# A fused attention and feed-forward kernel: a sixth split value tile, one side task in an earlier slot, and transposes moved from TensorE to DMA

## What is computed

```python
x = x + tanh(g_xattn) * attention(layernorm(x), ctx)
x = x + tanh(g_ffn) * ffn(layernorm(x))

# attention: 16 heads, everything through low-rank latents
q_big  = einsum(hidden_q @ Wq.T, w_kc_q)            # per head 384
q_r    = q_big @ W_qr;  k_r = rope(kv_c) @ W_kr     # per head 64
attn   = softmax(q_r @ k_r.T)                       # 512 x 1024 per head and batch
ctx_c  = attn @ rope(kv_c)                          # values are the 128-wide latents
out    = (ctx_c @ w_kc_kv) @ Wo.T

# ffn: three quantized products of 512 x 2048
xq = round(rmsnorm(x) * scale)     # int8 range, a scale per row
wq = round(tanh(w / mean|w|))      # -1, 0, 1
h  = silu(xq1 @ wq1.T) * (xq2 @ wq2.T)
y  = quant(rmsnorm(h)) @ wq3.T
```

## Time and profile before

| | |
|---|---|
| median of three runs | 655.0 us |
| the profiled execution, its own time | 656.19 us |
| its span, first to last instruction | 654.4 us |
| PE busy | 635.1 us, 97% |
| DVE busy | 536.5 us, 82% |
| ACT busy | 422.2 us, 65% |
| POOL busy | 360.2 us, 55% |
| granted TensorE clock | 1.000 throughout (the upper level, 2.4 GHz) |
| DMA: share of 16 engines in attention, in the feed-forward part | 0.77 to 0.83, 0.03 to 0.08 |

### The profile page before, as it was taken

One profiled execution on the slowest core, in us unless ns is written; L12 is line 12 of the kernel. 1 busy time (PEld: TensorE's weight loads), 2 busy tenths in 40 slices (PEclk: granted clock), 3 DMA queues, 4 the chain that ended last, 5 costly groups with the idle time before them and its releaser, 6 DMA issues.

```text
span 654.4 us, 9986 instructions
## 1 busy us (share of the span) xinstructions
PE 635.1 (97%) x2968; PEld 394.0 (60%) x2968; DVE 536.5 (82%) x870; ACT 422.2 (65%) x693; POOL 360.2 (55%) x304
## 2 busy tenths in 40 slices
PE   8789999999999999999999999999999998999997
PEld 7555466766766676666666666566656554545553
DVE  4778787788878877887789978997899987998863
ACT  2564686477737764776567766776666633598875
POOL 4722376655545554565367854664457144686651
PEclk9999999999999999999999999999999999999999
DMA  8207976788589858984988798878689872000001
GB/s 283 87 6 188 274 196 164 206 223 240 151 227 241 219 131 239 251 224 106 251 222 221 201 242 224 222 195 231 169 221 251 198 177 81 1 1 33 17 35 48
DMA packets 45208, 112.79 MB, mean 172 GB/s; under 512 B 11888, under 2 KB 15088, under 8 KB 45040
## 3 DMA queue, kind: packets, MB, share of 16 engines
q1 hardware_dynamic: 42128, 104.24, 60.1%
q10 hardware_dynamic: 2976, 8.06, 4.0%
q0 software_dynamic: 64, 0.00, 0.0%
HBM read 45.16 MB, written 2.10 MB: 72 GB/s over the span
## 4 chain that ended last, share of the span: by engine, by line
PE 68%; DVE 10%; SPq 8%; ACT 4%; issue 4%; DMA 3%; POOL 1%; PEld 1%; POOLq 0%; ACTq 0%; DVEq 0%; PEldq 0%
PE ps_s L1443 11%; SPq L1132 8%; PE ps_b L1476 6%; PE ps_s L623 5%; PE ps_ctx L1476 5%; PE ps_b L1339 4%; PE ps_b L1394 4%; DMA G<-E 3%; PE ps_b L1341 3%; PE ps_b L1413 3%; PE ps_b L1340 3%; ACT E L1675 2%; PE ps_b L674 2%; DVE small L1858 2%; PE ps_ctx L1472 2%
## 5 line engine op out<-in xcount | busy, mean ns | idle before, releaser
L1675 ACT ACTIVATE E<-ps_s,small 128x1024 f32<-128x1024 f32 x128 | 142.5, 1116 | 143.4 <-DVE small L1858 110.5
L1241 POOL TENSOR_TENSOR G_lo<-G,g_hi 128x512 fp32r<-128x512 f32 x130 | 168.0, 1306 | 117.7 <-ACT g_hi L1619 117.7
L1858 DVE TENSOR_REDUCE small<-ps_s 128x1 f32<-128x1024 f32 x128 | 149.8, 1211 | 34.5 <-PE ps_s L1443 34.3
L1872 DVE STREAM_TRANSPOSE E<-E 128x1024 f32<-128x1024 f32 x124 | 152.0, 1230 | 0.1
L1199 POOL TENSOR_SCALAR E<-E,small 128x1024 f32<-128x1024 f32 x64 | 78.9, 1233 | 109.6 <-DVE small L1864 98.0
L1619 ACT ACTIVATE g_hi<-G 128x512 fp32r<-128x512 f32 x130 | 76.9, 631 | 3.5 <-DVE wq L1888 3.5
L1339 PE MATMUL ps_b<-b_hi,ctx_hi 128*128 128x512 f32 x128 | 66.8, 522 | 0.3 <-DVE ctx_lo L1818 0.3
L1476 PE MATMUL ps_b<-G,kv 128*128 128x512 f32 x126 | 63.7, 600 | 1.7 <-DMA G<-E 1.7
L1476 PE MATMUL ps_ctx<-G,kv 128*128 128x512 f32 x126 | 64.6, 607 | 0.1
L1443 PE MATMUL ps_s<-k_hi,q_hi 64*128 64x512 f32 x256 | 57.3, 444 | 3.8 <-ACT E L1675 2.6
L623 PE MATMUL ps_s<-wq,q12T 128*128 128x512 fp8e4 x256 | 59.8, 379 | 0.1
(11 more groups left out here) (203 smaller groups left out, 1211.7 us busy)
## 6 DMA issues: line engine op xcount, KB each, us to landing
G<-E SPq DMA_DIRECT2D x496, 128.0 KB, 2.6
w_stage<-in_wffn SPq DMA_DIRECT2D x37, 512.0 KB, 4.8
w_stage<-in_wffn ACTq DMA_DIRECT2D x11, 512.0 KB, 4.4
wo_s<-in_woT SPq DMA_DIRECT2D x8, 512.0 KB, 5.4
wq_s<-in_wq SPq DMA_DIRECT2D x7, 512.0 KB, 5.5
wkcq_s<-in_wkcqT SPq DMA_DIRECT2D x7, 384.0 KB, 3.4
out<-x_sb SPq DMA_DIRECT2D x8, 256.0 KB, 2.0
x_sb<-in_x SPq DMA_DIRECT2D x3, 512.0 KB, 6.3
```

The costliest lines, as they stand in the source:

```text
L1241: nc.gpsimd.tensor_tensor(g_tile(w % 2, i, G_lo), tile, high_part(i).bitcast(F32).rearrange("p (t i q) -> p t i q", t=ST, i=4), ALU.subtra ...
L1675: nc.scalar.activation(out, scores, ACT.Exp, bias=negmax[:, k:k + 1], accum_out=rowsum[:, k:k + 1]).then_inc(exp_done, 1)
L1858: nc.vector.tensor_reduce(negmax[:, k:k + 1], ps_s[:, t % 2, :], AX_X, ALU.max, negate=True).then_inc(max_done, 1)
L1872: nc.vector.transpose(e_tile(w % 2, t), e_tile(w % 2, t)).then_inc(blocks_turned, 1)
```

## The change

- `SPLIT` is 6: tile 5 is split too, so that 26 more plain products become split ones. Tiles 6 and 7 are taken first. The fourth high part (index 3) is made at step 2 and no longer at step 3, that is between the exponentials of steps 2 and 3; GpSimd makes its low part before the second scaling. With six parts in three places, the wait for the unit before moves to part 2.
- The side task `("m",)` of pairs 1 to 6 moves to unit 2, step 2 of the pair before, as `("m", 1)`. `("a",)` moves from step 2 to step 0 of unit 0 and `("k", 1, 1)` from step 2 to step 0 of unit 2. Pair 0 does both `("m",)` and `("m", 1)`, pair 6 (`"late"`) and pair 7 none. VectorE takes the low part of a task of step 0 behind its two maxima for `("a",)` and `("k", 1, 1)` too, as it did for `q` (`behind`).
- SyncE no longer waits for `("m",)` at a pair's start (it finished a unit earlier), and waits after the exchange of unit 1 until it has landed (`landed`), before it issues the weight loads behind it. The weight sums of unit 1 stand at steps 3 and 4, not 1 and 4.
- In the feed-forward part the rows of tiles 2 to 7 and the hidden tiles 0 to 5 are transposed by DMA. ScalarE first converts int16 to bf16 in place (`widen_rows`, 128 x 1024; `widen_hidden`, 128 x 2048), then SyncE issues one transposing DMA. `down(t - 3)` follows chunk 1 of step `t`, in place of `down(t - 2)` at the end; the read of it stands ahead of the fourth product. The last two hidden tiles are still turned by TensorE.
- Small tiles are packed closer to make room, and the bf16 identity is made at the start.

```diff
-SPLIT, PLACES = 5, 3
-STEP_TILE = (5, 6, 0, 1, 7, 2, 3, 4)
-HIGH_STEPS = (0, 0, 0, 3, 4)
+SPLIT, PLACES = 6, 3
+STEP_TILE = (6, 7, 0, 1, 2, 3, 4, 5)
+HIGH_STEPS = (0, 0, 0, 2, 3, 4)
...
 SIDE = [
-    {0: ("m",), 2: ("a",), 3: ("k", 0, 0), 4: ("out", 3, 0), 5: ("out", 3, 1), 6: ("b", 0), 7: ("b", 1)},
+    {0: ("a",), 3: ("k", 0, 0), 4: ("out", 3, 0), 5: ("out", 3, 1), 6: ("b", 0), 7: ("b", 1)},
     {0: ("q", 0), 1: ("k", 0, 1), 4: ("out", 0, 0), 5: ("out", 0, 1), 7: ("k", 1, 0)},
-    {2: ("k", 1, 1), 4: ("out", 1, 0), 5: ("out", 1, 1)},
+    {0: ("k", 1, 1), 2: ("m", 1), 4: ("out", 1, 0), 5: ("out", 1, 1)},
     {0: ("q", 1), 4: ("out", 2, 0), 5: ("out", 2, 1)},
 ]
...
+        def landed(sp, p, w):
+
+            sp.wait_ge(exchanged[w % 2], 2 * EXCHANGE * p + EXCHANGE * (w // 2 + 1))
+            sp.sem_inc(sp_passed, 1)
...
                 if not (variant == "last" and w == 3):
                     exchange(sp, *unit_ahead(p, w, 1))
+                    if w == 0 and variant != "last":
+                        landed(sp, *unit_ahead(p, w, 1))
...
                 if splits(p, w):
                     split_low(pool, p, w, 2)
+                    split_low(pool, p, w, 3)
...
                 if splits(p, w):
-                    split_low(pool, p, w, 3)
                     split_low(pool, p, w, 4)
+                    split_low(pool, p, w, 5)
...
+            def turn_rows(t):
+                sp.wait_ge(q12_wide, t - FIRST_MOVED + 1)
+                sp.wait_ge(up_done, HC * (t - 1))
+                sp.dma_start_transpose(q12T[:, t % 2, :, :, :].rearrange("p i c s -> p (i c) s"),
+                                       qn12[:, t % 2, :, :].rearrange("p i d -> p (i d)").bitcast(BF16)).then_inc(q12_moved[t % 2], 16)
+
+            def turn_hidden(t):
+                sp.wait_ge(q3_wide, t + 1)
+                if t >= 2:
+                    sp.wait_ge(mm3_done, t - 1)
+                sp.dma_start_transpose(q3T[:, t % 2, :, :], qn3[:, t % 2, :].bitcast(BF16)).then_inc(q3_moved[t % 2], 16)
+
+            for t in range(1, TT):
+                if t + 1 < TT:
+                    turn_rows(t + 1)
+                if t >= 2:
+                    turn_hidden(t - 2)
+                if t >= 4:
+                    store(t - 4)
...
+        def widen_hidden(act, t):
+
+            act.wait_ge(q3_ready, t + 1)
+            rows = qn3[:, t % 2, :]
+            copy_act(rows.bitcast(BF16), rows).then_inc(q3_wide, 1)
...
                 if t == 1:
                     silu(act, 2, 0, 0)
+                    widen_hidden(act, 0)
                     norm_act(act, 2, 0)
-                elif mm:
+                else:
+                    widen_hidden(act, t - 1)
                     hidden_square(act, t, k)
...
                 if mm and t > 2:
                     product(dve, t, k, 2)
                     chunk_max(dve, t, k, 1)
+                    down_read(t - 3)
                     product(dve, t, k, 3)
```

More of the change, by code:

```diff
@@ L134 @@
 XN_JOIN_SLOTS = ((4, 1), (4, 2), (4, 3), (5, 0))
-def side_tasks(w, first, last):
-    def wanted(task):
-        before = task[:2] == ("out", 3)
-        behind = task[0] in ("m", "a", "k", "q")
-        return not (first and before or last and behind)
-    return {c: task for c, task in (LAST_SIDE_TASKS if last else SIDE)[w].items() if wanted(task)}
 PROLOGUE_TASKS = [("m",), ("a",), ("k", 0, 0), ("k", 0, 1), ("q", 0, 0), ("q", 0, 1), ("k", 1, 0), ("k", 1, 1), ("q", 1)]
@@ L1918, in dve_pair @@
                     ctx_low(dve, *((p, w - 1) if w else (p - 1, 3)))
-                if not queries:
+                if not behind:
                     low(1)
```

234 lines of the change are left out of this document (118 added, 116 removed).

## The result

| | before | the change |
|---|---|---|
| median | 655.1 us (four runs, 654.8 to 655.5) | 661.9 us (four runs, 658.2 to 665.0) |
| ratio | | 1.0109, 95% interval 1.0078 to 1.0139 |
| profiled execution, its span | 656.19, 654.4 us | 661.89, 660.1 us |
| granted TensorE clock of the four runs | 1.000 (profiled) | 0.992, 0.990, 0.997, 0.992 (at 661.9, 665.0, 658.2 and 662.0 us) |

What follows compares the result with a forecast made beforehand. TensorE was taken to bound, with VectorE close behind at `q` in attention and a four-engine loop nearly as long in feed-forward. Attention -5.2 and feed-forward +4.1 gave -1.1 on 656.2, 654.0 us on the median; range 650.3 to 664.

Steps and rivals of the forecast that it cites:

- Rival C: Feed-forward loop does not lengthen (term +1.5, not +4) or attention gives -7 to -9: 650 to 652.7 us; chance 0.27.
- TensorE idle 1 to 2 us a step: Expected sign in feed-forward tiles 3 to 5: TensorE waits this long, released by VectorE's products and not by a DMA.
- The copy between two exponentials makes the second of them some 0.5 us later: Attention, sixth split tile: ScalarE's extra copy delays an exponential; the 26 splits were to save TensorE 4.2 us.
- Rival B: Attention gives less: late low parts make 26 units wait 0.1 to 0.2 us each, attention -1, 656.5 to 659; chance 0.23.
- the join before pair 7: Join of six value tiles before attention's last pair: up to 0.9 us later, under VectorE's 2 us of work, costed at nothing.
- -3.0 for pair 2: Attention, pair 2 start to `q`: -1.6 as in other pairs, plus 1.4 us lost to the exchange of unit 1.
- `q` 17.5 us after the start: Attention, unit 1: TensorE's product `q` comes 17.5 us after the pair's start in place of 19.1, set by VectorE.
- +0.95 in unit 2: Attention, pairs 1 to 5: moved `m` adds 1.43 us on TensorE's path, the splits of three other units take 0.48.
- the lower bound of -9: Attention's best case if no wait is left at `q`: -5.2 less 4 x 0.4 and 2 x 1.1 us.
- the turns cost nothing: Feed-forward transposing DMAs: 4 to 5 us a row turn, 5 to 6 a hidden turn; up to 6 us a row turn is free.
- rival A: Slow row turns in SyncE's queue make `gate_up` wait for `q12T` from 6 us a turn on: 661 to 668 us; chance 0.20.
- The upper bound of attention: Attention's worst case: VectorE gains nothing in unit 0, `q` stays, unit 2 costs its 0.95 five times: about +4 us.

Runs made afterwards that it cites:

- c_ends: The change with plain instead of transposing transfers, down product behind the fourth chunk and its read at step end (not tile 7), widening ahead of the squares: 1.0099 of before.
- c_gaps: The change with plain transfers, down product and read at step ends, widening of hidden tiles 1 to 4 in halves behind second and third silu: 656.3 us, 1.0027 of before.
- c_widen_late: The change with plain transfers and the hidden widening moved behind the squares; the read stays ahead of the fourth product: 1.0113 of the kernel before.
- c_ends_wide: The change with plain transfers, the hidden widening behind the squares, and down product and read at the ends of their steps: 1.0176 of the kernel before.
- att_only: The kernel before with the changed attention and packed tiles, feed-forward part as before: 654.6 us, 0.9999 of the kernel before.
- att_again: The kernel before with the changed attention, feed-forward part as before, run once more on another chip: 654.6 us, 1.0000 of the kernel before.

## Why the prediction was wrong

The terms as forecast, and as the profile of the change has them against the one they were made on:

| term | forecast | measured |
|---|---|---|
| pairs 1 to 6, start to `q` | -10.6 | -9.1 |
| `q` to the next start, pairs 0 to 5 | +5.9 | +5.6 |
| behind the `q` of pair 6 | -0.5 | +1.5 |
| **attention** | **-5.2** | **-1.9** |
| first widening, tile 2 | +1.3, +1.4 | +1.4, +1.5 |
| tiles 3 to 5 | +2.0 | +3.5, of it 1.45 the clock |
| tile 6 | +1.1 | +3.05, of it 1.5 the clock |
| tile 7 | -1.7 | -1.8 |
| **feed-forward** | **+4.1** | **+7.7** |
| **sum on the profiled execution** | **-1.1** | **+5.7** (with 0.1 in what is left) |

- **Right: the mechanism of the feed-forward part.** Taking 8.1 us from TensorE gained nothing, because a loop over four engines was within 0.1 us of it; the change lengthened that loop to 12.2 us a tile, by the widening and by the early read. `c_ends` shows that the widening alone is enough (12.1), `c_gaps` that with both out the loop is back at 11.56. The early read alone comes to 12.2 by the 0.66 us between `c_widen_late` and `c_ends_wide`; no run has it by itself. Rival C, that it would not lengthen, fell.
- **Wrong: "TensorE idle 1 to 2 us a step" was costed at nothing.** The forecast saw the waits and asked only what they delay. The waits were 2.1 to 2.4 us, in one piece, at the first chunk of a tile. Behind three of them the clock fell, and behind two of these the step grew, by 1.45 and 1.51 us in the profiled execution. This is the larger part of what the feed-forward sum lacked (2.96 of 3.6 us).
- **Wrong: 'The copy between two exponentials makes the second of them some 0.5 us later', with GpSimd's extra subtraction costed at nothing because it waits for 45% of the time.** That is a share of the whole span. At four places the low part is the last thing that TensorE waits for, 0.4 to 1.1 us each. Rival B named this, with 0.1 to 0.2 us in each of 26 units and attention at -1; attention came to -1.9 by the trace, and to no gain in the time of `att_only` and `att_again`. It came as few waits in few units: 0.5 us in pair 1, 0.4 in pair 5, 1.6 in pair 6. Behind the `q` of pair 6 the forecast had -0.5, and it was +1.5.
- **Wrong: the join before pair 7, "up to 0.9 us later, under VectorE's 2 us of work".** TensorE waits 0.75 us for it. The forecast had it covered by VectorE's work, but the one who waits is TensorE.
- **Wrong: -3.0 for pair 2, carried over to the median.** Against the profiled execution it measured -2.9. But 1.4 of it was a wait for an exchange that the second trace of the same kernel does not have, so that it is no gain on the median. A transfer's delay in one pair out of three equal ones should have been read as that execution's.
- **Right by luck: `q` 17.5 us after the start** (17.6 in pairs 2 to 4, 18.4 in 5 and 6, and 18.4 in pair 1, which has 0.51 of waiting in it), +0.95 in unit 2 (0.8 to 1.1). But the forecast got it by following VectorE, put TensorE at `q` after 17.1, and kept a wait there. None is recorded but 0.07 to 0.08 us in pairs 5 and 6. The earlier trace rows have no wait in pair 1 either, so that TensorE's own 19.1 less 1.43 and 0.16 gives the same 17.5: the number was TensorE's, not VectorE's, and the lower bound of -9, made of waits to be removed, had nothing under it.
- **Right: the turns cost nothing.** 3.2 and 4.4 us, below the 4 to 5 and 5 to 6 taken, and both under their cover; rival A did not occur. The Trainium skill ("VectorE: DVE Perf Modes", The three transpose paths) gives 1309 ns a block; the trace has 8 blocks in 3.2 us and 16 in 4.4, so the blocks do not go one after another at that price. The Trainium skill's rule that a transposing DMA is as fast as a plain one ("Advanced Engine Details and Errata", X-Bar Transpose) is nearer, but not met here: 1.4 times as long.
- **Two slips of reckoning.** The upper bound of attention, "about +4", is 5 x 0.95 + 1.1 - 0.5 = +5.4 by its own terms. Rival A speaks of 18 separate block transposes a step; a step has 8 + 16 = 24 blocks, and 18 is the number of groups of eight in the whole part. Neither moved the sum.

So the sum missed by 6.8 us: 3.3 in attention, 3.6 in the feed-forward part, where all but 0.6 is the clock, and 0.1 the other way elsewhere. The time moved 6.8 us and the profiled executions 5.7; the other 1.1 is that the profile of before stood 1.2 over its median, about what the wait in pair 2 was worth, and that of the change on its own. The executions of the change lie 7 us apart, so its median too is known to about 2 us only.

## What to carry to other kernels

When two loops are equally long, work taken from one buys nothing, and the first thing to look up is what the change adds to the other: here a copy of 1.9 us that costs the loop nothing in two halves behind two silus, and 0.5 to 1.6 us a step at the two other places tried. Ask of each new wait of TensorE not only whom it delays but how long it is in one piece, since here waits of 2.1 us and more were often followed by products at half speed. And price from a share of busy time only what has no deadline; for an operation that the bound engine waits for, follow its own queue in the tightest unit, and in a second trace if there is one.
